# A selective-scan kernel: ScalarE copies the carry of a scan step behind the next step's second exponential

## The chip, the cores and the metric

One core of one Trainium2 chip runs the whole program. The metric is device microseconds (us) of one execution; shown are the median of three runs and one execution with a profile.

## What is computed

A sandwich of three residual blocks on x, four sequences of 1024 tokens by 512 channels, in fp32: half a gated feed-forward (512 to 1408 to 512, ternary weights), a Mamba block, and the same feed-forward again, each on a layer norm of its input. The Mamba block holds the recurrence that the change touches:

```
def step(s, inp):                        # over the 1024 tokens of a sequence
    u_t, d_t, B_t, C_t = inp
    dA = jnp.exp(d_t[..., None] * A)     # 1024 channels x 16 states
    dBu = d_t[..., None] * B_t[:, None, :] * u_t[..., None]
    s = dA * s + dBu
    y = jnp.einsum('bin,bn->bi', s, C_t)
    return (s, y)
```

Around it stand an input projection to 2048 channels, a convolution over four tokens with silu, a small projection for the step size, B and C with RMS norms, softplus, the gate, and the output projection.

## The kernel before

**Chunks.** The 4096 tokens are eight chunks of 512 (`TC`); two chunks make one sequence. An even chunk (0, 2, 4, 6) opens a sequence and its states start at zero; an odd chunk continues it and starts from the states at which the even one ended. These are the carries: `carry` holds one column for each of the 16 states n and 8 channel blocks.

**Scan steps.** The scan of a chunk is 32 steps (`Book.scan`, line 897, made into instructions by the functions named below): `ig`, one of two groups of four channel blocks, by `n`, one of 16 states. A step is, by engine:
- GpSimd (`pool_scan`, L1883): two products of 128x1024, `dus` by the broadcast row `bring`, into `sbuf[:, s3]`, one of three state buffers.
- ScalarE (`act_scan`, L1512): four exponentials of 128x512 (k = 0 to 3), from `dls` into PSUM, `pa[k % 2]`. There are two `pa` banks, so exponential k waits for scan k-2; the first of a step waits for scan 2 of the step before, the second for its scan 3.
- VectorE (`dve_scan`, L1684): four scans of 128x512 (`tensor_tensor_scan`, L1691), each over `pa[k % 2]` and the product, in place in `sbuf`. In an even chunk the start value is the constant 0.0, in an odd one a column of `carry`; the profile shows them as two forms.
- ScalarE again, in even chunks alone (L1522): one copy of the last column of the four results, 128x4, into `carry`. It waits for scan 3 of its own step (`q.wait_ge(u.scan[3], ...)`, L1521) and stands, in the list of the thread, between exponential 3 of its step and exponential 0 of the next.
- TensorE (`pe_states`, L1361): 16 transposes of 128x128 from `sbuf` into `pt` (two banks), after scan 3.
- Then the sum over n: VectorE adds `pt` by a column of `cT` to `acc` (L1702); for n = 4, 8, 12 ScalarE scales into `tmp` (L1538) and GpSimd adds (L1903); for n = 0 ScalarE writes `acc`.

A scan of an odd chunk waits for `u.carry_in` (L1943), the token `sfree["carry"]`: the last copy booked so far, thus the last one of the whole even chunk. A state buffer comes free when its transposes and its copy are done (L981).

**Order of the work.** Beside the scan run the stages of other chunks: `ffn1`, `prep_in`, `post`, `ffn2`, softplus (`dt0` to `dt3`), in rounds (`ROUND`, `NEST`). Each engine's work is given as threads (`m` main, `c` convolution, `l` norms, `d` softplus, `s` scan, `t` states, `z` setup), each with a fixed order of its own. `Plan.order` (L189) merges the threads of all engines when the kernel is built: with a model of durations it takes, again and again, the instruction that could start first, so that the order in every queue, of the DMA issues (SP) too, follows from the model and from what each thread waits for. On the chip each queue runs in that order and waits where a semaphore is not yet there. `Lane.wait_ge` leaves out a wait whose value the same engine has waited for already.

Of the kernel before, what the change touches and what calls it, by code (L numbers as in the profile page):

```python
# [8 lines left out]
TC = 512  # L9
# [41 lines left out]
ACT = mybir.ActivationFunctionType  # L51
# [26 lines left out]
class Unit:  # L78


    def __init__(self, kind, c=None):
        self.kind = kind
        self.c = c
# [170 lines left out]
class Book:  # L254
# [3 lines left out]
    def __init__(self, sems, light):  # L258
        self.S = sems
        self.light = light  # L260
        self.n = {}
        self.setup = None
        self.lists = {}
        self.pieces = {}
        self.raw_no, self.raw_free = 0, [()] * 4
        self.part_free = [()] * 4
        self.bank_no, self.bank_free, self.held = 0, [()] * NM, set()
        self.free, self.sfree = {}, {}
        self.norm_out, self.rows_in, self.rows_out = {}, {}, {}
        self.direct = {}  # L270
        self.early = {}
        self.following = None
        self.slot_free = [()] * SLOTS
        self.slot_at = 0
        self.ring_tok = {}
        self.first_half = True
        self.small = None
        self.check = None
        self.stores = []
        self.scans, self.turns, self.softs = 0, 0, 0  # L280
        self.first_stage()

    def up(self, sem, by=1):
# [613 lines left out]
    def scan(self, c):  # L897
        S = self.S
        sf = lambda name: self.sfree.get(name, ())
        second = c % 2 == 1  # L900
        d_tok, u_tok = {}, {}

        def load_d(ig, k):
            if (c, ig) == (0, 0):
                d_tok[ig, k] = self.delta[c, k][0]
                return
            u = self.add("dl_in", Unit("dl", c))
            u.i, u.k, u.before = 4 * ig + k, k, (self.delta[c, 4 * ig + k][0],) + sf(("dl", k))
            u.there = d_tok[ig, k] = self.up(S.l_dl[k], 16)

        def load_u(ig, k):
            if (c, ig) == (0, 0):
                u_tok[ig, k] = self.delta[c, k][1]
                return
            u = self.add("du_in", Unit("du", c))
            u.i, u.k, u.before = 4 * ig + k, k, (self.delta[c, 4 * ig + k][1],) + sf(("du", k // 2))
            u.there = u_tok[ig, k] = self.up(S.l_du[k], 16)

        for k in range(4):
            load_d(0, k)  # L920
            load_u(0, k)
        for g in range(2 * N):
            u = self.add("s", Unit("scan", c))
            u.g, u.ig, u.n = g, g // N, g % N
            u.s2, u.s3, u.second = self.scans % 2, self.scans % 3, second
            self.scans += 1
            v = self.add("bb_in", Unit("b", c))
            v.n, v.s2, v.before = u.n, u.s2, (self.b_there[c],) + sf(("b", u.s2))
            u.b_there = v.there = self.up(S.l_b[u.s2], 16)
            u.du_there = [u_tok[u.ig, k] for k in range(4)]  # L930
            u.dl_there = [d_tok[u.ig, k] for k in range(4)]
            u.st_before = sf(("sb", u.s3))
            u.prod = []
            for h in range(CUT):
                u.prod.append(self.up(S.g_dbu))
                if u.n == N - 1:
                    self.sfree["du", h] = (u.prod[h],)
                    if u.ig == 0:
                        load_u(1, 2 * h)
                        load_u(1, 2 * h + 1)  # L940
            self.sfree["b", u.s2] = (u.prod[-1],)
            u.pa_before, u.exp, u.scan = [], [], []
            u.carry_in = sf("carry") if second else ()
            for k in range(4):
                u.pa_before.append(sf(("pa", k % 2)))
                u.exp.append(self.up(S.a_exp))
                if u.n == N - 1:
                    self.sfree["dl", k] = (u.exp[k],)
                    if u.ig == 0:
                        load_d(1, k)  # L950
                u.scan.append(self.up(S.v_scan))
                self.sfree["pa", k % 2] = (u.scan[k],)
            if second:
                self.sfree["carry_rd"] = (u.scan[3],)
                u.carry = ()
            else:
                u.carry_before = sf("carry_rd")
                u.carry = (self.up(S.a_carry),)
                self.sfree["carry"] = u.carry
            self.add("t", u)  # L960
            u.ct = self.x_small[c].ct
            u.pt, u.pt_before, u.tr, u.acc_before, u.mul, u.sum = [], [], [], [], [], []
            u.tmp_before = []
            for tt in range(4):
                b = self.turns % NT
                self.turns += 1
                u.pt.append(b)
                u.pt_before.append(sf(("pt", b)))
                u.tr.append(self.up(S.p_sc))
                u.acc_before.append(sf("acc") if u.n == 0 else sf(("acc", u.ig, tt)))  # L970
                if u.n in SHARED:
                    u.mul.append(self.up(S.a_cmul))
                    u.tmp_before.append(sf("tmp"))
                    u.sum.append(self.up(S.g_cadd))
                    self.sfree["tmp"] = (u.sum[tt],)
                else:
                    u.mul.append(self.up(S.a_cmul if u.n == 0 else S.v_cmac))
                    u.sum.append(u.mul[tt])
                self.sfree["pt", b] = (u.mul[tt],)
                self.sfree["acc", u.ig, tt] = (u.sum[tt],)  # L980
            self.sfree["sb", u.s3] = (u.tr[3],) + u.carry  # L981
            if u.n == N - 1 and (c, u.ig) == (NCH - 1, 1):
                self.y_ready[c, 1] = u.sum[3]
            elif u.n == N - 1:
                u.y_kept = self.y_ready[c, u.ig] = self.up(S.st_y[u.ig], 16)
                self.add("y_out", u)
                self.sfree["acc"] = (u.y_kept,)
        self.sfree["cT", c % 4] = (u.sum[3],)
# [115 lines left out]
def macaron(nc, x_in, wp_in, wx_in, wdt_in, const_in, lnw_in, ds_in, ident_in, out):  # L1104
    ctx = ExitStack()
    with ctx:
        def sb(name, shape, dt=F32):
            return ctx.enter_context(nc.sbuf_tensor(name, shape, dt))
# [60 lines left out]
        sbuf = sb("sbuf", [P, 3, 4, TC])  # L1169
        acc = sb("acc", [P, 4, 512])  # L1170
        dsb = sb("dsb", [P, H])
        carry = sb("carry", [P, N, NI])
# [6 lines left out]
        S = Unit("semaphores")  # L1179
# [39 lines left out]
        def col(i, n=1):  # L1219
            return cst[:, i:i + n]  # L1220
# [291 lines left out]
        def act_scan(units):  # L1512
            def program(q, e):
                for u in units:
                    for k in range(4):
                        q.wait_ge(u.dl_there[k], *u.pa_before[k])
                        e.activation(pa[k % 2][:, :], dls[:, k, :], ACT.Exp,  # L1517
                                     scale=col(C_A + (4 * u.ig + k) * N + u.n)).then_inc(S.a_exp, 1)
                        yield
                    if not u.second:  # L1520
                        q.wait_ge(u.scan[3], *u.carry_before)  # L1521
                        e.activation(carry[:, u.n, 4 * u.ig:4 * u.ig + 4], sbuf[:, u.s3, :, TC - 1],  # L1522
                                     ACT.Copy).then_inc(S.a_carry, 1)
                        yield
            return program

        def act_states(units):
# [707 lines left out]
```

## Time and profile before

| | |
|---|---|
| median of 3 runs | 2909.91 us (2907.37 to 2915.78) |
| profiled execution, its own time | 2897.91 us |
| its span | 2896.1 us |
| busy: VectorE / TensorE / GpSimd / ScalarE | 86% / 84% / 78% / 61% |
| mean granted TensorE clock | 0.909 |

The span is the time from the first to the last instruction; the profiled execution's own time is 1.8 us longer. The shares are busy time over the span. TensorE's matmuls are pipelined and their ends are modelled, so its share is not a distance to a limit. In the rows PE is TensorE, PEld its weight loads, DVE VectorE, ACT ScalarE, POOL GpSimd; "idle before" is the time that the engine stood still just before an instruction, and the arrow names what ended it.

### The profile page before, as it was taken

What the parts mean: (1) busy time and instruction counts of PE and PEld (TensorE: products, weight loads), DVE (VectorE), ACT (ScalarE), POOL (GpSimd) and SP (SyncE); (2) the same over time, 40 slices, a digit from 0 to 9 for tenths busy, and PEclk for the clock granted to TensorE, in tenths of its full rate; (3) what the DMA queues carried; (4) which work ended last, traced back from release to release, by engine and by line L of the source; (5) the groups of instructions that cost most, each with busy time, mean ns of one, the idle gap of its engine ahead of it and who ended that gap; (6) DMA issues with size and microseconds to landing.
All of it is one profiled execution on the core that took longest, in us unless ns stands there. A gap on an engine that the chain in (4) does not pass through costs nothing. (4 is left out here: it accounts for less than half of the span.)

```text
span 2896.1 us, 38161 instructions
## 1 busy us (share of the span) xinstructions
PE 2419.9 (84%) x12266; PEld 1961.3 (68%) x12266; DVE 2496.7 (86%) x3131; ACT 1756.8 (61%) x2995; POOL 2259.9 (78%) x1370
## 2 busy tenths in 40 slices
PE   6678879788777998889988899889988896599968
PEld 5466667667665876677766777667766775377757
DVE  5549899799889999899989988798988888999973
ACT  5447568667466665576657665667656667465522
POOL 2237859988976889689997889779896799889852
PEclk9869889899888999899998999889999897599989
DMA  7635573673677467945777366854678378355544
GB/s 269 238 114 167 178 241 107 224 264 121 234 263 260 116 201 254 323 163 186 230 266 285 121 223 226 309 206 149 219 253 289 130 260 307 105 194 189 189 163 142
DMA packets 293951, 606.65 MB, mean 209 GB/s; under 512 B 23024, under 2 KB 23792, under 8 KB 293744
## 3 DMA queue, kind: packets, MB, share of 16 engines
q1 hardware_dynamic: 293744, 604.13, 62.1%
q8 instruction: 101, 1.65, 0.2%
q14 instruction: 106, 0.87, 0.1%
HBM read 451.47 MB, written 152.57 MB: 209 GB/s over the span
## 5 line engine op out<-in xcount | busy, mean ns | idle before, releaser
L1890 POOL TENSOR_TENSOR sbuf<-dus,bring 128x1024 f32<-128x1024 f32 x512 | 1220.9, 2400 | 235.0 <-PE pt L1367 130.3
L1517 ACT ACTIVATE pa<-dls,cst 128x512 f32<-128x512 f32 x1024 | 691.5, 688 | 425.8 <-DVE sbuf L1691 419.2
L1367 PE MATMUL pt<-ident,sbuf 128*128 128x128 f32 x4096 | 660.8, 298 | 230.2 <-DVE sbuf L1691 99.8
L1367 PEld LDWEIGHTS pt<-ident,sbuf 128*128 128x128 f32 x4096 | 513.7, 152 | 392.4 <-DVE sbuf L1691 140.6
L1287 PE MATMUL pm<-xT,wring 128*128 128x512 f32 x2816 | 705.7, 399 | 10.7 <-DVE xT L1574 4.3
L1691 DVE TENSOR_TENSOR_SCAN sbuf<-pa,sbuf 128x512 f32<-128x512 f32 x512 | 608.6, 1211 | 65.6 <-ACT pa L1517 55.7
L1691 DVE TENSOR_TENSOR_SCAN sbuf<-pa,carry,sbuf 128x512 f32<-128x512 f32 x512 | 635.0, 1269 | 25.8 <-ACT pa L1517 19.5
L1702 DVE SCALAR_TENSOR_TENSOR acc<-pt,cT,acc 128x512 f32<-128x512 f32 x768 | 548.5, 739 | 78.4 <-PE pt L1367 74.9
L1299 PE MATMUL pm<-wring,act 128*128 128x512 f32 x2176 | 579.7, 409 | 33.2 <-DMA wring<-wsp 11.2
L1287 PEld LDWEIGHTS pm<-xT,wring 128*128 128x128 f32 x2816 | 516.8, 189 | 113.4 <-issue 14.2
L1310 PE MATMUL pm<-xT,wring 128*128 128x512 f32 x1536 | 427.8, 430 | 74.2 <-DVE hd L1641 29.5
L1299 PEld LDWEIGHTS pm<-wring,act 128*128 128x128 f32 x2176 | 401.4, 193 | 120.7 <-DVE hd L1619 16.0
L1310 PEld LDWEIGHTS pm<-xT,wring 128*128 128x128 f32 x1536 | 308.1, 208 | 148.0 <-issue 56.3
L1765 POOL TENSOR_TENSOR act<-hd,act 128x512 fp32r<-128x512 f32 x240 | 310.2, 1298 | 116.6 <-ACT act L1400 115.7
L1903 POOL TENSOR_TENSOR acc<-acc,tmp 128x512 f32<-128x512 f32 x192 | 248.1, 1292 | 45.5 <-ACT tmp L1538 45.1
L1400 ACT ACTIVATE act<-hd 128x512 fp32r<-128x512 f32 x240 | 149.1, 623 | 89.1 <-DVE hd L1619 71.7
L1538 ACT ACTIVATE tmp<-pt,cT 128x512 f32<-128x512 f32 x192 | 130.9, 682 | 89.2 <-POOL acc L1903 76.4
L1396 ACT ACTIVATE th<-pm,csh 128x512 f32<-128x512 f32 x176 | 119.9, 681 | 84.6 <-PE pm L1287 84.0
L1579 DVE SCALAR_TENSOR_TENSOR aa<-th,pm 128x512 f32<-128x512 f32 x176 | 118.1, 671 | 50.4 <-ACT th L1396 50.0
L1323 PE MATMUL pm<-wxs,act 128*128 128x160 f32 x768 | 131.8, 332 | 19.4 <-DVE hd L1641 19.4
L1583 DVE SCALAR_TENSOR_TENSOR hd<-aa,csh,pm 128x512 f32<-128x512 f32 x176 | 129.8, 738 | 17.1 <-PE pm L1287 12.5
L1806 POOL TENSOR_TENSOR act<-hd,act 128x512 fp32r<-128x512 f32 x64 | 82.1, 1283 | 74.9 <-ACT act L1458 69.8
(129 smaller groups left out, 2286.1 us busy)
## 6 DMA issues: line engine op xcount, KB each, us to landing
wring<-wsp SPq DMA_DIRECT2D x408, 512.0 KB, 4.6
bring<-b_d SPq DMA_DIRECT2D x256, 256.0 KB, 4.0
xn_d<-tb SPq DMA_DIRECT2D x24, 1024.0 KB, 9.6
xnb<-xn_d SPq DMA_DIRECT2D x19, 1024.0 KB, 7.4
x_d<-tb SPq DMA_DIRECT2D x16, 1024.0 KB, 6.0
u_d<-hd SPq DMA_DIRECT2D x64, 256.0 KB, 4.5
sg_d<-hd SPq DMA_DIRECT2D x64, 256.0 KB, 4.0
tb<-x_d SPq DMA_DIRECT2D x16, 1024.0 KB, 7.0
```

Source lines behind the costliest of these rows:

```text
L1287: ins = e.matmul(pm[b][:, :], wring[:, slot, up if light else pw, k * P:(k + 1) * P], xT[:, px, k, :], start=(pw, px, k) == (0, 0, 0), sto ...
L1299: ins = e.matmul(pm[u.bank[tt]][:, :], act[:, px, u.k, tt * P:(tt + 1) * P], wring[:, u.slot, pw + u.half, :], start=u.first and (pw, px) ...
L1310: ins = e.matmul(pm[u.bank][:, :], wring[:, u.slot, pw, k * P:(k + 1) * P], xT[:, px, k, :], start=(pw, px, k) == (0, 0, 0), stop=end)
L1323: ins = e.matmul(pm[u.bank[tt // 2]][:, (tt % 2) * XW:(tt % 2 + 1) * XW], act[:, pw, u.k, tt * P:(tt + 1) * P], wxs[:, px, u.k, :], start= ...
L1367: ins = e.matmul(pt[u.pt[tt]][:, k * P:(k + 1) * P], sbuf[:, u.s3, k, tt * P:(tt + 1) * P], ident[:, :], is_transpose=True, start=True, st ...
L1400: e.activation(act[:, 0, u.k, :], hd[:, u.h, :], ACT.Copy).then_inc(S.a_hi, 1)
L1517: e.activation(pa[k % 2][:, :], dls[:, k, :], ACT.Exp, scale=col(C_A + (4 * u.ig + k) * N + u.n)).then_inc(S.a_exp, 1)
L1691: e.tensor_tensor_scan(d, pa[k % 2][:, :], d, init, ALU.mult, ALU.add).then_inc(S.v_scan, 1)
L1702: e.scalar_tensor_tensor(acc[:, tt, :], pt[u.pt[tt]][:, :], cT[:, u.c % 4, tt, u.n:u.n + 1], acc[:, tt, :], ALU.mult, ALU.add).then_inc(S. ...
L1765: e.tensor_tensor(act[:, 1, u.k, :], hd[:, u.h, :], act[:, 0, u.k, :], ALU.subtract).then_inc(S.g_lo, 1)
L1890: e.tensor_tensor(sbuf[:, u.s3, h * m:(h + 1) * m, :], dus[:, h * m:(h + 1) * m, :], bring[:, u.s2:u.s2 + 1, :].broadcast_to([P, m, TC]), ...
L1903: e.tensor_tensor(acc[:, tt, :], acc[:, tt, :], tmp[:, :], ALU.add).then_inc(S.g_cadd, 1)
```

## The change

The copy of a step is issued inside the next step, behind its second exponential (k = 1), whether that step belongs to the same chunk or is the first of the odd chunk. `behind` carries the unit of the step before along. Each scan step of an odd chunk now waits for the copy of its own `ig` and `n` rather than for the last copy of the even chunk.

```
@@ Book.__init__
         self.scans, self.turns, self.softs = 0, 0, 0
+        self.carried, self.behind = {}, None
         self.first_stage()
@@ Book.scan
             u.pa_before, u.exp, u.scan = [], [], []
-            u.carry_in = sf("carry") if second else ()
+            u.carry_in = self.carried[u.ig, u.n] if second else ()
+            u.behind = self.behind
             for k in range(4):
                 u.pa_before.append(sf(("pa", k % 2)))
                 u.exp.append(self.up(S.a_exp))
@@
             if second:
                 self.sfree["carry_rd"] = (u.scan[3],)
-                u.carry = ()
+                u.carry, self.behind = (), None
             else:
                 u.carry_before = sf("carry_rd")
-                u.carry = (self.up(S.a_carry),)
-                self.sfree["carry"] = u.carry
+                u.carry = self.carried[u.ig, u.n] = (self.up(S.a_carry),)
+                self.behind = u
             self.add("t", u)
@@ act_scan
                         e.activation(pa[k % 2][:, :], dls[:, k, :], ACT.Exp,
                                      scale=col(C_A + (4 * u.ig + k) * N + u.n)).then_inc(S.a_exp, 1)
                         yield
-                    if not u.second:
-                        q.wait_ge(u.scan[3], *u.carry_before)
-                        e.activation(carry[:, u.n, 4 * u.ig:4 * u.ig + 4], sbuf[:, u.s3, :, TC - 1],
-                                     ACT.Copy).then_inc(S.a_carry, 1)
-                        yield
+                        if k == 1 and u.behind:
+                            v = u.behind
+                            q.wait_ge(v.scan[3], *v.carry_before)
+                            e.activation(carry[:, v.n, 4 * v.ig:4 * v.ig + 4], sbuf[:, v.s3, :, TC - 1],
+                                         ACT.Copy).then_inc(S.a_carry, 1)
+                            yield
```

## Rows read from the trace of the kernel before

**Rows 1.** The page's head: the span, and each engine's busy time.

```profile
span 2896.1 us, 38161 instructions
...
PE 2419.9 (84%) x12266; PEld 1961.3 (68%) x12266; DVE 2496.7 (86%) x3131; ACT 1756.8 (61%) x2995; POOL 2259.9 (78%) x1370
```

**Rows 2.** Busy time by stretch; a row is the scan of chunks 0 to 7.

```profile
core 0: us, PE busy (x) PEld busy (x) DVE busy (x) ACT busy (x) POOL busy (x), PEclk, DMA share, GB/s
207.00:535.00 328.00, 275.97 (x1413) 223.87 (x1413) 293.03 (x351) 210.22 (x384) 252.71 (x146) 0.92 0.54 179
535.00:888.00 353.00, 280.66 (x1403) 225.30 (x1404) 323.96 (x400) 230.40 (x373) 297.13 (x183) 0.89 0.67 229
888.00:1217.00 329.00, 288.36 (x1512) 235.08 (x1510) 297.50 (x377) 205.39 (x371) 276.99 (x166) 0.93 0.66 216
1217.00:1536.00 319.00, 284.10 (x1495) 230.33 (x1494) 296.10 (x369) 209.54 (x340) 282.71 (x174) 0.95 0.67 224
1536.00:1880.00 344.00, 302.53 (x1564) 246.11 (x1563) 302.38 (x383) 222.72 (x398) 285.79 (x170) 0.93 0.67 227
1880.00:2210.00 330.00, 293.56 (x1528) 236.87 (x1527) 301.61 (x371) 209.10 (x340) 283.13 (x171) 0.94 0.67 222
2210.00:2520.00 310.00, 232.97 (x1185) 190.24 (x1184) 268.87 (x319) 202.50 (x358) 271.62 (x153) 0.83 0.61 208
2520.00:2790.00 270.00, 241.59 (x1250) 191.43 (x1248) 265.18 (x309) 151.90 (x234) 231.77 (x131) 0.93 0.59 192
```

**Rows 3.** VectorE's groups by form: odd chunks' scans, then even chunks'.

```profile
line engine op names shapes xcount | busy us, mean ns | idle before us <-releasers
L1691 DVE TENSOR_TENSOR_SCAN sbuf<-pa,carry,sbuf 128x512 f32<-128x512 f32 x512 | 635.0, 1269 | 25.8 <-ACT pa L1517 19.5 <-POOL sbuf L1890 5.7
L1691 DVE TENSOR_TENSOR_SCAN sbuf<-pa,sbuf 128x512 f32<-128x512 f32 x512 | 608.6, 1211 | 65.6 <-ACT pa L1517 55.7 <-POOL sbuf L1890 9.1
```

**Rows 4.** VectorE's waits (us, times, longest), one row from each stretch, chunks 0 to 7.

```profile
DVE sbuf L1691 <- ACT pa L1517: 10.4, 14, 2.9
...
DVE sbuf L1691 <- ACT pa L1517: 6.4, 7, 1.5
...
DVE sbuf L1691 <- ACT pa L1517: 14.5, 19, 1.6
...
DVE sbuf L1691 <- ACT pa L1517: 8.6, 4, 3.7
...
DVE sbuf L1691 <- ACT pa L1517: 15.9, 17, 3.6
...
DVE sbuf L1691 <- ACT pa L1517: 3.5, 5, 1.5
...
DVE sbuf L1691 <- ACT pa L1517: 14.9, 15, 5.0
...
DVE sbuf L1691 <- ACT pa L1517: 1.0, 2, 0.9
```

**Rows 5.** Timeline, all engines, at a step's end in chunk 2 (start, length in us).

```profile
1110.36 2.33 DVE L1691 TENSOR_TENSOR_SCAN sbuf<-pa,sbuf 128x512 f32<-128x512 f32 x2
...
1112.72 0.21 ACT L1522 ACTIVATE carry<-sbuf 128x4 f32<-128x4 f32 x1 [2.85 <-DVE sbuf L1691]
...
1112.83 1.29 ACT L1517 ACTIVATE pa<-dls,cst 128x512 f32<-128x512 f32 x2
1113.54 1.22 DVE L1691 TENSOR_TENSOR_SCAN sbuf<-pa,sbuf 128x512 f32<-128x512 f32 x1 [0.85 <-ACT pa L1517]
```

**Rows 6.** Timeline of VectorE in chunk 3: seven scans, over a step's end.

```profile
1444.49 8.33 DVE L1691 TENSOR_TENSOR_SCAN sbuf<-pa,carry,sbuf 128x512 f32<-128x512 f32 x7
```

**Rows 7.** Timeline of VectorE in chunk 2: a step's end with other work behind it.

```profile
1090.48 1.22 DVE L1691 TENSOR_TENSOR_SCAN sbuf<-pa,sbuf 128x512 f32<-128x512 f32 x1
1091.62 0.72 DVE L1583 SCALAR_TENSOR_TENSOR hd<-aa,csh,pm 128x512 f32<-128x512 f32 x1
1092.56 1.22 DVE L1691 TENSOR_TENSOR_SCAN sbuf<-pa,sbuf 128x512 f32<-128x512 f32 x1 [0.22 <-ACT pa L1517]
```

**Rows 8.** The copy's own line: its durations, what it waits for, who waits for it.

```profile
L1522 ACT ACTIVATE carry<-sbuf x128: 190/208/238, 214.8 to 2519.5; 128x4 f32<-128x4 f32 x128
...
  DVE sbuf L1691: 135.6, 79
...
  POOL sbuf L1890: 0.3, 1
```

**Rows 9.** GpSimd's products: idle time before them, and what ended it.

```profile
L1890 POOL TENSOR_TENSOR sbuf<-dus,bring 128x1024 f32<-128x1024 f32 x512 | 1220.9, 2400 | 235.0 <-PE pt L1367 130.3 <-issue 41.9 <-DMA bring<-b_d 34.4
```

## The prediction

> **What bounds the kernel now.** I read the page's head first [rows 1]: VectorE is busiest, 2496.7 us of a span of 2896.1, so 399 us of it are idle; TensorE and GpSimd are not far behind. A mean hides where the idle time lies, so I cut the span at the starts of the eight scans [rows 2]. In the odd chunks VectorE is idle 353-324.0, 319-296.1, 330-301.6 and 270-265.2 us, together 85.1. In the even ones it is idle 328-293.0, 329-297.5, 344-302.4 and 310-268.9 us, together 149.2. Even chunks thus carry 64.1 us more idle time, though each holds the same 128 scans. The reader has a natural experiment here: the scan of an even chunk and that of an odd one differ in little but the carry copy. The scans by form say the same [rows 3]: 65.6 us idle before the 512 even ones, 25.8 before the 512 odd ones, and nearly all of the difference was ended by an exponential (55.7 against 19.5 us). By stretch [rows 4] that wait is 10.4, 14.5, 15.9 and 14.9 us in even chunks (65 times) and 6.4, 8.6, 3.5 and 1.0 us in odd ones (18 times): an excess of 55.7-19.5 = 36.2 us.
>
> The timeline shows how one such wait is made [rows 5]. The last scan of the step ends at 1110.36+2.33 = 1112.69. ScalarE has stood still for 2.85 us in front of the copy; it starts 0.03 us later, at 1112.72, the next exponential only at 1112.83, and VectorE's next scan at 1113.54, after 0.85 us of nothing. The exponential itself needed only the scan before the last one. In the odd chunk [rows 6] seven scans run over a step's end in 8.33 us: (8.33-1.27)/6 = 1.18 us from start to start, no hole. Where VectorE has other work at a step's end, the hole is partly filled: with one operation of 0.72 us between, 0.22 us are left [rows 7].
>
> **The change, part by part.**
>
> *Exponential 0 no longer waits for scan 3.* It moves to the end of scan 2, some 1.2 us earlier, and needs under 0.7 us (two back to back take 1.29 [rows 5]): it is done before scan 3 ends. This takes the hole out. Three prices: nothing, if another wait takes its place; the exponential waits' excess, 36.2 us [rows 4]; all excess idle time of VectorE in even chunks, 64.1 us [rows 2], if TensorE and the sums also come on time because the scans do. I take the middle one, since it is the only one that the waits name, and lower it below.
>
> *Exponential 1* waits for scan 3 before and after, but now starts 0.03 us after its end instead of about 0.03+0.11+0.65 us. Scan 0 of the next step then runs for 1.21 us [rows 3] while exponential 1 takes 0.7: it hides.
>
> *The copy* costs 0.21 us by its own row [rows 8], but the next exponential starts 0.11 us after it [rows 5], so it takes 128 x 0.11 = 14 us of ScalarE. Its own wait has been met by exponential 1's, so 135.6 us of ScalarE standing before the copy [rows 8] turn into standing before exponentials 1 and 2. Exponential 1 ends about 0.03+0.7 us after scan 3, the copy leaves the engine at some 0.85, exponential 2 may start once scan 0 is done, at 1.2: 0.3 us of cover, more where VectorE has other work between. Cost nothing; with the cover gone, the 14 us. Queued behind the copy are exponentials 2 and 3, and `tmp`, tanh and the casts where the planner puts them.
>
> *State buffers.* The copy, now about 0.7 us later, also frees a buffer for the product three steps on. GpSimd waited for a copy once, 0.3 us [rows 8], but 130.3 us for the transposes that free the same buffer [rows 9] and come later than the copy. Nothing.
>
> *Odd chunks.* Each of 32 steps now tests a semaphore for its own copy, 128 tests instead of 4, on VectorE's queue. Every copy was made a whole chunk earlier, but for the first steps, and the last copy of an even chunk, now behind exponential 1 of the odd one, is needed 31 steps later. Bounds: nothing, since a step's first scan, which tests two semaphores, comes at the same 1.18 us as the others [rows 6]; or 124 x 0.03 = 4 us, if each costs what the copy took to start [rows 5]. I take nothing. Nothing is moved past a DMA; the SP queue changes only as the merge does.
>
> *The merge.* `Plan.order` runs over other waits, so all queues may be ordered anew. No row prices this. Two odd chunks of like work differ by 22.9 against 28.4 us of idle VectorE [rows 2]: 5.5 us a stretch, 5.5 x sqrt(8) = 16 us over eight if signs are random. I take zero, and 16 us either way.
>
> *What is late next.* The time given back is kept only where other engines follow. The highest shares that any stretch reaches are 0.891 for TensorE (284.1/319) and 0.886 for GpSimd (282.7/319) [rows 2]. If those are ceilings, chunk 2 can shrink only to 288.4/0.891 = 323.6 (5.4 us), chunk 4 to 302.5/0.891 = 339.5 (4.5), chunk 6 to 271.6/0.886 = 306.6 (3.4), and chunk 0, far from both, keeps its excess over an odd chunk's mean, 10.4-4.9 = 5.5. That makes 18.8 us. They are shares reached, not limits, so I take the middle of 36.2 and 18.8: 27.5, say **28 us**.
>
> Sum: 2897.9-28 = 2869.9 us for the profiled execution. The median of the runs stood 12.0 us above it, so I forecast 2909.9-28 = **2882 us**, 1.0% faster.
>
> **The rivals.**
>
> *Kept in full, and more.* VectorE in even chunks gets as tight as in odd ones: -64 us, 2846. For: ScalarE no longer blocks tanh and casts while it stands before the copy. Against: the waits name only 36 us of it, and chunk 7, with 4.8 us idle, flatters the odd side. 9%.
>
> *Another engine takes it.* The ceilings hold and the merge eats some: -5 us, 2905. For: TensorE at 0.88 in chunks 2 and 4, GpSimd at 0.88 in chunk 6. Against: chunk 3 runs at 0.89 on TensorE, 0.93 on VectorE and 0.89 on GpSimd together. 18%.
>
> *The hole is a shortage of banks.* Two `pa` banks serve four exponentials; if they were the cause, the copy would only stand beside it, and nothing would change: 2910. The same two banks serve the odd chunk, where there is no hole [rows 6]. 4%. The Trainium skill, Perfetto Trace Analysis, Optimization Strategy, says that one and the same gap, again and again on the engine that should be saturated, can mean that SBUF or PSUM has no room for the next tile. By that rule the 0.85 us would stay; the trace does not agree with it.
>
> *Slower: the scan pushes in front of the main work.* The hole served other threads: the feed-forward's and the convolution's VectorE operations slipped in at a step's end [rows 7]. Now the next scan is ready at once, and the merge, which takes what can start first, lets them wait 1.21 us longer; TensorE stands without their results. At 23 step ends of 128 where TensorE truly stands for it, 23 x 1.21 = 28 us, the gain is gone; at 40 it is 48 us against 28: +20, 2930. For: most even step ends do have other work behind them (65 waits in 128). Against: odd chunks have just this order, and are no longer for it. 7%.
>
> **How the numbers follow.** The forecast's own case has 62%, its range -28 with 16 us for the merge and some 6 more for the ceilings: 2860 to 2904. The range reaches down into the better rival to 2850 and up over the ceilings' case to 2908; outside are the slower rival, the banks' case, about half of the better one and a little of the tails, some 18%. A change of 0.3%, 8.7 us, is about what a measurement of this kernel can tell from none: its three runs span 8.4 us. Faster by more: nearly all of the 62%, the 9%, a quarter of the 18%: 0.75. Within: the rest of it, the banks, a little of the forecast's: 0.18. Slower: 0.07.
>
> **What would show it.** In the changed kernel: exponential waits before even scans fall from 55.7 us to about 20; no wait of ScalarE before the copy, and 100 us or more of it in front of exponentials; two scans over an even step's end start 1.13 us apart; even chunks 0, 2, 4, 6 each 5 to 10 us shorter, odd ones unchanged within 6. Against me: a hole of the same size ended by an exponential (banks); VectorE's waits for transposes or TensorE's for VectorE growing by what the scans gave back (another engine); longer waits of TensorE before `pm` matmuls for `hd` or `xT` (slower).

## The result and the profile after

The changed kernel takes 2927.5 us, median of 6 runs (2919.2 to 2936.6), against 2907.6 for the kernel before (6 runs, 2903.9 to 2915.8). The ratio is 1.0060, 95% interval 1.0037 to 1.0083: slower by 0.6%, where 1.0% faster was forecast. Its profiled execution took 2923.08 us.

The head of its page, with the words of [rows 1]:

```profile
span 2921.3 us, 38167 instructions
...
PE 2434.4 (83%) x12266; PEld 1973.0 (68%) x12266; DVE 2491.9 (85%) x3131; ACT 1757.9 (60%) x2995; POOL 2260.7 (77%) x1370
```

The work is the same; VectorE is even busy 5 us less (2491.9 against 2496.7). The time lost is idle time. VectorE's groups by form, as in [rows 3], show that the change did what it says:

```profile
L1694 DVE TENSOR_TENSOR_SCAN sbuf<-pa,carry,sbuf 128x512 f32<-128x512 f32 x512 | 635.0, 1268 | 61.2 <-POOL sbuf L1893 39.0 <-ACT pa L1519 15.8 <-issue 6.0
L1694 DVE TENSOR_TENSOR_SCAN sbuf<-pa,sbuf 128x512 f32<-128x512 f32 x512 | 604.2, 1206 | 50.9 <-POOL sbuf L1893 38.8 <-ACT pa L1519 11.4
```

Idle time ended by an exponential before even scans fell from 55.7 to 11.4 us, 44 us less, more than the 36 forecast. In its place stands another: waits for GpSimd's products, 77.8 us in all against 14.8 (5.7 and 9.1 in [rows 3]). Before all scans together VectorE is idle 112.1 us, where it was 91.4. At a step's end in chunk 6, VectorE (first fence) and ScalarE (second) now look like this:

```profile
2311.23 5.66 DVE L1694 TENSOR_TENSOR_SCAN sbuf<-pa,sbuf 128x512 f32<-128x512 f32 x5
```

```profile
2312.47 0.69 ACT L1519 ACTIVATE pa<-dls,cst 128x512 f32<-128x512 f32 x1 [0.42 <-DVE sbuf L1694]
2313.58 0.69 ACT L1519 ACTIVATE pa<-dls,cst 128x512 f32<-128x512 f32 x1 [0.42 <-DVE sbuf L1694]
2314.21 0.19 ACT L1525 ACTIVATE carry<-sbuf 128x4 f32<-128x4 f32 x1
2314.69 0.69 ACT L1519 ACTIVATE pa<-dls,cst 128x512 f32<-128x512 f32 x1 [0.29 <-DVE sbuf L1694]
```

Five scans run on over the step's end, 1.11 us apart, where [rows 5] had a hole of 0.85. The copy waits for nothing, and ScalarE still stands idle for 0.29 us between it and exponential 2: the cover of 0.3 us was sized right.

The stretches by scan, chunks 0 to 7, beside [rows 2]:

```profile
210.00:532.00 322.00, 260.65 (x1346) 209.94 (x1345) 295.45 (x354) 212.17 (x385) 244.32 (x141) 0.92 0.53 173
532.00:899.00 367.00, 295.94 (x1468) 236.91 (x1466) 319.70 (x398) 230.62 (x372) 305.98 (x188) 0.90 0.67 228
899.00:1194.00 295.00, 263.65 (x1377) 214.74 (x1376) 274.86 (x334) 190.86 (x348) 258.31 (x151) 0.92 0.59 196
1194.00:1555.00 361.00, 320.40 (x1624) 260.37 (x1623) 315.94 (x403) 220.54 (x356) 298.05 (x184) 0.91 0.68 228
1555.00:1869.00 314.00, 273.31 (x1432) 222.25 (x1431) 284.17 (x351) 209.79 (x381) 270.00 (x160) 0.93 0.65 217
1869.00:2211.00 342.00, 301.64 (x1553) 245.03 (x1552) 306.00 (x384) 211.01 (x341) 289.26 (x177) 0.93 0.67 223
2211.00:2544.00 333.00, 256.39 (x1291) 207.98 (x1290) 281.12 (x347) 216.56 (x381) 280.36 (x160) 0.84 0.67 222
2544.00:2815.00 271.00, 239.88 (x1254) 191.41 (x1252) 266.97 (x312) 151.02 (x232) 236.27 (x133) 0.94 0.60 193
```

Even chunks went from 328+329+344+310 = 1311 to 322+295+314+333 = 1264 us, 47 less; odd ones from 353+319+330+270 = 1272 to 367+361+342+271 = 1341, 69 more. Look at TensorE's column too: in chunk 2 it is busy 263.7 us against 288.4, in chunk 3 320.4 against 284.1. The scans of even chunks ran ahead and left work of other chunks' stages behind, and it was made up later. VectorE's idle time went from 149.2 to 128.4 us in even chunks and from 85.1 to 132.4 in odd ones.

Up to the scan of chunk 6 these shifts cancel: it begins at 2210 us in the kernel before and at 2211 in the changed one. Chunk 6 itself then takes 333 us for 310, which is nearly all of the 25 us between the two spans. In that stretch VectorE waits 26.7 us for products, against 3.9 before.

Where the scans stand: five waits of VectorE, one row from each of five timelines.

```profile
555.11 1.28 DVE L1694 TENSOR_TENSOR_SCAN sbuf<-pa,carry,sbuf 128x512 f32<-128x512 f32 x1 [19.32 <-POOL sbuf L1893]
...
1387.17 2.46 DVE L1694 TENSOR_TENSOR_SCAN sbuf<-pa,carry,sbuf 128x512 f32<-128x512 f32 x2 [7.49 <-POOL sbuf L1893]
...
1728.46 2.34 DVE L1694 TENSOR_TENSOR_SCAN sbuf<-pa,sbuf 128x512 f32<-128x512 f32 x2 [8.98 <-POOL sbuf L1893]
...
2065.90 1.28 DVE L1694 TENSOR_TENSOR_SCAN sbuf<-pa,carry,sbuf 128x512 f32<-128x512 f32 x1 [8.66 <-POOL sbuf L1893]
...
2399.18 3.53 DVE L1694 TENSOR_TENSOR_SCAN sbuf<-pa,sbuf 128x512 f32<-128x512 f32 x3 [13.57 <-POOL sbuf L1893]
```

Together 58 of the 77.8 us. Each is scan 2 of the first step of a group of four channel blocks: the scan that needs the second pair of blocks of its group. In chunk 1 it is the first group, and the pair comes from softplus' part 1; in the four others it is the second group, and the pair comes from softplus' last part, 3. The last of the five on GpSimd's timeline and then on the DMA queue's (SP):

```profile
2379.21 2.39 POOL L1830 TENSOR_TENSOR spw<-spx,spw 128x1024 f32<-128x1024 f32 x1
...
2396.74 6.95 POOL L1893 TENSOR_TENSOR sbuf<-dus,bring 128x1024 f32<-128x1024 f32 x3 [9.09 <-DMA dus<-du_d]
```

```profile
2381.63 0.36 SPq L2071 DMA_DIRECT2D du_d<-spw  x1
...
2388.18 1.23 SPq L2087 DMA_DIRECT2D dus<-du_d  x2
```

Softplus' product ends at 2381.60, is stored, loaded again, and the scan's product starts at 2396.74, 15.1 us later. In the kernel before that store was issued 33 us sooner, though the scan of chunk 6 began at the same time (2210 and 2211):

```profile
2348.71 0.36 SPq L2068 DMA_DIRECT2D du_d<-spw  x1
```

So the trace offers two stories: the scans were made faster and run into softplus' results, or the new merge is simply a worse one. The merge is new indeed: going through the two traces in order, by operation and tiles, 1881 of VectorE's 3131 instructions differ from the one at the same place before, and 5576 of TensorE's 12266 weight loads. The experiments take the two stories apart.

### The profile page after: what moved, and what is told of

Its sections match the earlier page's. It is cut to its first block and busy times, and to the rows that moved or that the text cites. A ratio compares the mean times of both kernels' runs of the same rounds, so it can differ in the third digit from the quotient of the medians.

```text
span 2921.3 us, 38167 instructions
## 1 busy us (share of the span) xinstructions
PE 2434.4 (83%) x12266; PEld 1973.0 (68%) x12266; DVE 2491.9 (85%) x3131; ACT 1757.9 (60%) x2995; POOL 2260.7 (77%) x1370
## 5 line engine op out<-in xcount | busy, mean ns | idle before, releaser
L1519 ACT ACTIVATE pa<-dls,cst 128x512 f32<-128x512 f32 x1024 | 699.6, 691 | 574.1 <-DVE sbuf L1694 537.3
L1301 PE MATMUL pm<-wring,act 128*128 128x512 f32 x2176 | 573.8, 407 | 37.0 <-DMA wring<-wsp 10.4
L1289 PEld LDWEIGHTS pm<-xT,wring 128*128 128x128 f32 x2816 | 519.7, 191 | 120.2 <-issue 20.5
L1768 POOL TENSOR_TENSOR act<-hd,act 128x512 fp32r<-128x512 f32 x240 | 311.2, 1303 | 120.0 <-ACT act L1402 118.6
L1325 PEld LDWEIGHTS pm<-wxs,act 128*128 128x128 f32 x768 | 124.3, 249 | 15.7 <-DVE hd L1644 8.0
```

What stands on the lines that cost most here:

```text
L1289: ins = e.matmul(pm[b][:, :], wring[:, slot, up if light else pw, k * P:(k + 1) * P], xT[:, px, k, :], start=(pw, px, k) == (0, 0, 0), sto ...
L1301: ins = e.matmul(pm[u.bank[tt]][:, :], act[:, px, u.k, tt * P:(tt + 1) * P], wring[:, u.slot, pw + u.half, :], start=u.first and (pw, px) ...
L1325: ins = e.matmul(pm[u.bank[tt // 2]][:, (tt % 2) * XW:(tt % 2 + 1) * XW], act[:, pw, u.k, tt * P:(tt + 1) * P], wxs[:, px, u.k, :], start= ...
L1519: e.activation(pa[k % 2][:, :], dls[:, k, :], ACT.Exp, scale=col(C_A + (4 * u.ig + k) * N + u.n)).then_inc(S.a_exp, 1)
L1768: e.tensor_tensor(act[:, 1, u.k, :], hd[:, u.h, :], act[:, 0, u.k, :], ALU.subtract).then_inc(S.g_lo, 1)
```

## The experiments

Ratios are against the kernel before on the same chip; intervals are 95%. MARGIN and LAND are constants of the merge's model alone: changing one changes the order of the queues and none of their work.

**The change in the old order.** The merge sees the scan thread as before, the engines get the changed one. Four queues hold the same work in the same order as in the kernel before (VectorE's scans of odd chunks have the change's waits); on ScalarE, exponentials 0 and 1 take the places one earlier, and the copy the place that exponential 1 had.

```
+def form(e):
+    return "old" if isinstance(e, Sketch) else "new"
...
-                        q.wait_ge(u.exp[k], u.prod[k * CUT // 4], *u.carry_in)
+                        q.wait_ge(u.exp[k], u.prod[k * CUT // 4], *u.carry_in[form(e)])
...
-                        if k == 1 and u.behind:
+                        if form(e) == "new" and k == 1 and u.behind:
...
+                    if form(e) == "old" and not u.second:
+                        q.wait_ge(u.scan[3], *u.carry_before)
+                        e.activation(carry[:, u.n, 4 * u.ig:4 * u.ig + 4], sbuf[:, u.s3, :, TC - 1],
+                                     ACT.Copy).then_inc(S.a_carry, 1)
+                        yield
```

> The copy behind exponential 1 and the waits of the change, but every queue merged as before the change; only ScalarE's scan thread has its copy two places later. Theory A (the hole is worth what the waits said; the changed kernel lost it to the new merge): 15 to 36 us faster than before, exponential waits before even scans down from 55.7 us to under 25, no long wait for products. Theory B (the hole was covered, the copy's new place is itself no gain or a loss): within 6 us of before or slower. Theory C (the softplus results bound the scans of a block group whatever the order): waits for products grow here too, to 30 us or more, and the time is within 6 us of before.

Measured: 2908.1 us, ratio 0.9986 (0.9967 to 1.0006). Its forms:

```profile
L1703 DVE TENSOR_TENSOR_SCAN sbuf<-pa,sbuf 128x512 f32<-128x512 f32 x512 | 607.2, 1211 | 47.5 <-ACT pa L1523 33.5 <-POOL sbuf L1902 13.0
L1714 DVE SCALAR_TENSOR_TENSOR acc<-pt,cT,acc 128x512 f32<-128x512 f32 x768 | 551.3, 743 | 92.7 <-PE pt L1373 88.4 <-POOL acc L1915 2.0
```

18 us less idle time before even scans (47.5 for 65.6), exponential waits 33.5 rather than under 25, no long waits for products, and 4 us of time that the interval does not tell from nothing. Theory A fell, C too; B holds. In this one execution the sums of VectorE waited 92.7 us, 88.4 of them for transposes; the page of the kernel before has 74.9 us for those. The two other orders below don't repeat that (68.0 to 65.6 and 63.5 to 65.2 us), so where the rest of the idle time went stays open. The loss of 20 us is not there at all: it belongs to the new order.

The same in two other orders, those that the kernel before gets with MARGIN at 0.28 and 0.32:

```
-MARGIN = 0.3
+MARGIN = 0.28
```

> The copy behind exponential 1 and the change's waits, in the order of the kernel before at MARGIN 0.28 (2930, ratio 1.0073). Theory S (the changed dependence by itself is worth almost nothing in a given order; the 20 us are the merge's draw): ratio 1.003 to 1.009. Theory A (the hole is worth something where the order is not the one it was fitted to): under 1.001, 18 us or more below 2930.

> The same in the order of the kernel before at MARGIN 0.32 (2926, ratio 1.0056). Theory S: ratio 1.001 to 1.007. Theory A: under 0.999.

Measured: 1.0045 (1.0024 to 1.0066) where that order had 1.0073 with the old copy, and 1.0035 (1.0018 to 1.0053) where it had 1.0056. The even scans in both orders, old copy and new, MARGIN 0.28 first:

```profile
L1691 DVE TENSOR_TENSOR_SCAN sbuf<-pa,sbuf 128x512 f32<-128x512 f32 x512 | 608.7, 1210 | 94.9 <-ACT pa L1517 68.3 <-POOL sbuf L1890 26.0
```

```profile
L1703 DVE TENSOR_TENSOR_SCAN sbuf<-pa,sbuf 128x512 f32<-128x512 f32 x512 | 606.6, 1208 | 76.8 <-ACT pa L1523 47.6 <-POOL sbuf L1902 28.1
```

```profile
L1691 DVE TENSOR_TENSOR_SCAN sbuf<-pa,sbuf 128x512 f32<-128x512 f32 x512 | 609.0, 1210 | 106.0 <-ACT pa L1517 70.9 <-POOL sbuf L1890 34.7
```

```profile
L1703 DVE TENSOR_TENSOR_SCAN sbuf<-pa,sbuf 128x512 f32<-128x512 f32 x512 | 607.0, 1209 | 86.1 <-ACT pa L1523 50.4 <-POOL sbuf L1902 34.3
```

Both ratios lie where Theory S had them, and Theory A fell twice. Exponential waits fall by 22, 21 and 20.5 us in the three orders, and the time by 0.14, 0.28 and 0.21%: 4, 8 and 6 us. None of the three steps is clear by itself; that all have one sign and one size is the evidence. Taken together they are 0.21%, give or take some 0.15% (an estimate from the intervals of the single ratios). In a given order the change is worth about 6 us, less than a third of the idle time it removes.

**Is the loss a draw of the merge?** MARGIN at 0.28 and 0.32, then 0.29 and 0.31, on both kernels.

> The kernel before, with a constant of the merge's model (MARGIN, the spare time it wants between one engine's result and another's use) at 0.28 us in place of 0.30: the same work, merged a little differently. Theory S (the loss of 20 us is a draw of the merge): this one, its partner at 0.32 and the two on the changed kernel scatter by 15 us or more, with no order between the two families. Theory M (the changed dependence makes the merge worse in itself): both of the changed family are 10 us or more above both of this one.

> The changed kernel with MARGIN at 0.28. Theory S: anywhere from 2890 to 2930. Theory M: 2915 or more, with long waits of the scans for products at a block group.

> The kernel before with MARGIN at 0.32. Theory S: 15 us or more away from its partner at 0.28 or from 2908. Theory M: within 8 us of 2908.

> The changed kernel with MARGIN at 0.32. Theory S: anywhere from 2890 to 2930. Theory M: 2915 or more.

> The kernel before with MARGIN at 0.29. Theory L (0.30 is a lucky order of the kernel before, the changed kernel never had it): ratio to before 1.003 or more, like 0.28 (1.0073) and 0.32 (1.0056). Theory M (the changed dependence merges worse): within 0.3% of before, the two others being strays.

> The changed kernel with MARGIN at 0.29. Theory L: on average no more than 5 us above its partner on the kernel before, either sign. Theory M: 10 us or more above its partner.

> The kernel before with MARGIN at 0.31. Theory L: ratio 1.003 or more. Theory M: within 0.3% of before.

> The changed kernel with MARGIN at 0.31. Theory L: within 10 us of its partner, either sign. Theory M: 10 us or more above its partner.

Measured (medians in us, and ratios):

| MARGIN | kernel before | changed kernel |
|---|---|---|
| 0.28 | 2930.2, 1.0073 (1.0051 to 1.0095) | 2929.3, 1.0075 (1.0045 to 1.0104) |
| 0.29 | 2925.0, 1.0049 (1.0025 to 1.0073) | 2932.6, 1.0073 (1.0049 to 1.0097) |
| 0.30 | 1 | 2927.5, 1.0060 (1.0037 to 1.0083) |
| 0.31 | 2937.0, 1.0078 (1.0054 to 1.0103) | 2928.2, 1.0055 (1.0036 to 1.0075) |
| 0.32 | 2926.4, 1.0056 (1.0034 to 1.0078) | 2933.5, 1.0088 (1.0059 to 1.0116) |

The one order of this table that stands out is the kernel before's own, at 0.30. Any of four small disturbances costs it 0.5 to 0.8%, as much as the change does. Theory L holds: the change took away a good order. The traces hint at where: the scan of chunk 6 takes 310 us in the kernel before (307 in the old order with the new copy), but 352, 351 and 347 us at 0.28, 0.31 and 0.32; at 0.29 it takes 310 too, and chunk 4 374 for 343.

Theory S asked for a scatter of 15 us or more among the disturbed kernels, and that is not there: the eight lie from 2925 to 2937 us. Theory M, put as a gap of 10 us between the two families, is not seen: the pairs differ by +0.02, +0.24, -0.23 and +0.32%, and the means are 1.0064 and 1.0073, 0.09% or 3 us apart. Each family scatters by 0.14%, so four members of each leave that difference open from about -0.15 to +0.33% (an estimate), and 10 us lies just at its edge.

But equal totals hide two effects. Where the same change was measured in the old order too, one can go from left to right: first the change alone, then the merge anew. VectorE's waits in us, first for exponentials, then for products:

| MARGIN | kernel before | the change in the old order | changed kernel, merged anew |
|---|---|---|---|
| 0.28 | 1.0073; 80.2, 41.9 | 1.0045; 60.4, 42.6 | 1.0075; 27.9, 75.9 |
| 0.30 | 1; 75.2, 14.8 | 0.9986; 56.3, 16.2 | 1.0060; 27.2, 77.8 |
| 0.32 | 1.0056; 81.4, 55.2 | 1.0035; 60.0, 54.0 | 1.0088; 29.2, 88.8 |

The last step costs 0.30, 0.74 and 0.53% (the first of them not clear by itself): some 12 us even at 0.28 and 0.32, where no good order was lost. With it the waits for products grow by 33 to 62 us; all five merges of the changed kernel have 72 to 89 us of them, the four disturbed ones of the kernel before 35 to 55. So the rows say that with the new dependence the merge places the scans where they run into late products, and that this gives back the 6 us that the change is worth in a given order. It rests on two merges beside the one at 0.30, and that these waits are what the new merge costs is argued from the rows, not isolated by a run.

**Do softplus' results hold the scans?** In chunks 1 to 7 the scans load blocks 0 and 1 in place of 2 to 7: the same transfers, other data, so the output is another; what goes is the need for softplus' later parts.

```
-            u.i, u.k, u.before = 4 * ig + k, k, (self.delta[c, 4 * ig + k][0],) + sf(("dl", k))
+            i = k % 2 if c else 4 * ig + k
+            u.i, u.k, u.before = i, k, (self.delta[c, i][0],) + sf(("dl", k))
```

and the same for the products.

> The kernel before, but in chunks 1 to 7 the scans load the step sizes and products of blocks 0 and 1 in place of blocks 2 to 7 (same sizes and number of loads, other data), so that no scan waits for the later parts of softplus. Theory A (in the kernel before the scans hardly wait for these parts): within 10 us of before. Theory C: also within 10 us, since only a faster scan meets them. Rival D (the scan is always held by them): 20 us or more faster.

> The same edit on the changed kernel. If its loss comes from scans that reach a block group before softplus has stored it (58 us of VectorE's waits for products at five such places), the waits at these places vanish and it is 20 us or more faster than the changed kernel's 2927, at or below the kernel before with the same edit. If the loss lies in the main work that the scans push back, it stays within 10 us of 2927.

> The kernel before with early blocks (loads of blocks 0 and 1 in place of 2 to 7 in chunks 1 to 7), at MARGIN 0.32. Theory B (softplus results hold a scan made faster: the change is worth 20 us where they don't): within 10 us of the same edit at 0.30 (2903), and 12 us or more above its partner on the changed kernel. Theory S: anywhere from 2885 to 2930.

> The changed kernel with early blocks at MARGIN 0.32. Theory B: within 10 us of 2883, at least 12 us below its partner on the kernel before. Theory S: within 8 us of its partner, or above it.

Measured: at 0.30 the kernel before 2903.1 (0.9957, 0.9942 to 0.9973) and the changed one 2882.9 (0.9889, 0.9874 to 0.9905); at 0.32 2882.6 (0.9900, 0.9866 to 0.9935) and 2895.0 (0.9933, 0.9911 to 0.9956). VectorE's waits for products in the changed kernel at 0.30, 77.8 us before the edit:

```profile
DVE sbuf L1696 <- POOL sbuf L1895: 26.5, 14, 6.8
```

The kernel before gained 9 us (medians side by side), as two of its theories had it, and Rival D fell; the changed kernel gained 45 us, more than the 20 asked for. This first pair alone spoke for Theory B, that the change is worth 20 us once softplus is out of the way; the second pair reversed the sign, so B fell. What the four runs share is that all are faster than the same kernel and MARGIN without the edit, by 0.4, 1.7, 1.6 and 1.5%. Without the need for softplus' later parts either kernel gains more than the hole costs: some 40 to 50 us in the three orders tried beside the good one. The edit changes what threads wait for, so each of these runs also has a merge of its own; the disturbed merges above scatter by far less than 40 us.

**Softplus parts nested earlier**, on the changed kernel:

```
-    NEST["post", c - LAG] = {3: ("dt1", c - 1)}
-    NEST["prep_in", c] = {4: ("dt2", c - 1)}
-    NEST["ffn2", c - LAG] = {4: ("dt3", c - 1)}
+    NEST["post", c - LAG] = {0: ("dt1", c - 1)}
+    NEST["prep_in", c] = {1: ("dt2", c - 1)}
+    NEST["ffn2", c - LAG] = {0: ("dt3", c - 1)}
```

> The changed kernel with softplus parts 1, 2, 3 nested earlier in post, prep_in and ffn2 (at 0, 1, 0 in place of 3, 4, 4) for chunks from 3 on. If the scans' waits at block groups are the loss: 10 to 30 us faster than the changed kernel, with waits for products under 40 us. If the main work pushed back is the loss: no faster than the changed kernel, maybe slower, since VectorE and ScalarE have the same work.

Measured: 2933.4 us, 1.0063 (1.0047 to 1.0078), like the changed kernel. Of its waits:

```profile
DVE sbuf L1694 <- POOL sbuf L1893: 46.3, 19, 17.7
DVE tb L1603 <- PE pm L1301: 42.9, 5, 13.3
```

The waits for products fell by 31 us, to 46.3 and not under the 40 named, and waits of VectorE for TensorE before the feed-forward's outputs came in their place: 42.9 us, against 10.8 in the changed kernel. The time didn't move, so the second expectation held. A new merge is part of this run too.

**A merge that expects transfers to take longer**, on both:

```
-ISSUE, LAND = 0.42, 2.5
+ISSUE, LAND = 0.42, 5.0
```

> The changed kernel with the model's time from the end of a DMA issue's transfer to its landing (LAND) at 5.0 us in place of 2.5, nearer to the 3 to 8 us that the stores and loads of softplus' results take in the trace, so that the merge puts other work ahead of a scan whose block group has not come back from memory. Theory G (the hole's gain is given back at the block groups because the merge believes the results are there): waits of scans for products under 50 us, ratio 1.002 or less. Rival (the results are late because softplus itself is behind the main work, not because of the round trip): waits for products stay at 60 us or more, ratio 1.005 or more.

> The same edit on the kernel before, as the control. Theory G: ratio 1.000 to 1.006, 5 us or more above its partner on the changed kernel, because the hole is still there. Rival: ratio 1.003 to 1.009, equal to its partner.

Measured: the changed kernel 2900.5 us, 0.9964 (0.9947 to 0.9981); the kernel before 2909.3, 0.9987 (0.9970 to 1.0003). The changed kernel with this constant is faster than both kernels, by 0.36% and about 1.0%. Theory G had this ratio right, but its waits for products are as long as ever, so it named a wrong reason; the rival had the waits right and the ratio wrong. The control's 0.9987 lies outside what either gave it.

```profile
DVE sbuf L1694 <- POOL sbuf L1893: 75.5, 26, 24.2
DVE aa L1582 <- ACT th L1398: 61.6, 45, 4.1
DVE acc L1705 <- PE pt L1369: 47.0, 58, 4.7
```

The partners differ by 0.23%, 7 us, which their intervals do not quite tell from nothing. Why 5.0 merges better is open: it is one draw too for each kernel, though both drew well. It does show that 0.30 is not the only good order, and that the changed kernel has one as well.

## Why the prediction was wrong

*The hole, and what closes it.* Right in its mechanism: exponential 0 is ready, the copy waits for nothing and is covered, the odd chunks' 128 tests and the state buffers cost nothing that shows. The waits before even scans fell from 55.7 to 11.4 us, under the 20 named. But half of that fall is the new merge's: in the old order they fell to 33.5, by 22 us and not by 36. Of the other signs, ScalarE's waits before exponentials grew by 118 us, as put. The even chunks did not each shrink by 5 to 10 us (-6, -34, -30, +23), and the odd ones did not stay within 6 (+14, +42, +12, +1).

*"What is late next", sized at 8 us of 36.* This step failed first: it kept 28 us. In one and the same order 20 to 22 us of exponential waits are gone and 4 to 8 us of time are kept. I treated VectorE's wait as the bound of even chunks, since it was the busiest engine, and took the ceilings of the others from shares of busy time. That a scan which starts 0.85 us sooner mostly waits at the next place where other engines come in is the likely reason; no run shows the place. The natural experiment compared idle time, not how fast the rest could follow: the ceilings alone (18.8 us) were nearer than the waits' sum and still three times too high.

*"The merge. I take zero, and 16 us either way."* This is the step that turned the sign. A symmetrical price supposed that the order of the kernel before is a typical one. It is a good one: four neighbours of it lie 14 to 23 us higher (0.49 to 0.78% of 2910). Measured directly, from the change in the old order (0.9986) to the changed kernel (1.0060), the term taken as zero is 0.74%, 21 us. By the neighbours it has two parts, a good order lost, some 19 us, and some 12 us that the new dependence costs in the merge; less the 6 us of the change that makes +25, against +17 measured by the ratio (an estimate, each part good to several us). The range had to reach at least to 2909.9+19-6 = 2923. The idle time of two odd chunks in one profile said nothing about it, because both come from the same order.

*The slower rival* came nearest with its time, 2930 at 7%, and in part by luck. Scans pushing in front of the other stages' work is what the profile shows, and the new dependence does cost something in the merge. But most of the 20 us is the good order lost, which the rival didn't have, and it priced 40 step ends at which TensorE stands, which no run shows. Its 65 waits in 128 are waits that exponentials ended and do not count step ends; that most of these have other work is true all the same, 94 of the 124 inside even chunks in the trace of the kernel before. That the scan's lead ran into softplus (58 us at five places) was in no rival. It is real and holds both kernels in most orders, the changed one for longer.

*Rivals of no change.* The banks are excluded: the hole closed with the same two `pa` banks. *Another engine takes it*, at -5 us, was right in size for a given order; which engine is not shown.

*The 12 us between the profiled execution and the median* I carried along as a constant. The kernel before has shown medians of 2907.6 to 2913.8 in the batches since, and 2907.6 beside the changed kernel: 2 of the 45 us of error, and on the other side.

## What to carry to other kernels

Where a program merges all queues from a model, an edit to one dependence is two changes: the dependence, and a new order for everything. Price them apart: issue the edit in the old order, and disturb the model's constants by a few per cent on both kernels to see how far orders scatter and where today's lies among them. Equal totals of two such families do not say that nothing happened: look at the waits, and at the fixed-order run between them. An idle gap on the busiest engine is an upper bound of the gain; what is kept depends on who else has slack at that very place, and a comparison of two stretches of one profile does not show it.

## What the runs showed beside this

A change of 0.01 us in one constant of the merge's model moves the median of the kernel before by 0.5 to 0.8%; medians of one and the same kernel differ by 0.2% from batch to batch, though single executions span up to 0.8% in a batch. The changed kernel, which had no good order to lose at 0.30, moves by 0.13 and 0.05% for the same 0.01 us either way. And a result that goes through memory between two engines, small as it is (512 KB stored and loaded), came back 15.1 us after it was made, 2381.60 to 2396.74, where the median of this pair's transfers over the kernel is 4.7 us from issue to landing. The store of 512 KB landed 5.5 us after its issue; the loads of 256 KB were issued at 2388.18, behind others in the same queue, and landed after 7.8 us, in a stretch (2381 to 2397) in which the core's DMA engines were 95% busy.
